# Building the token table: three buffers of 0/1 matrices, comparisons on pairs of fp16 values, and the narrow matrix ahead of the wide one

## The reference

```python
logits = xf @ gate_w.T + lb_bias
scores = sigmoid(logits); topw, topi = top_k(scores, 2)
topw = topw / (topw.sum(-1) + 1e-8)
for e in range(8):
    m = topi == e; sel = m.any(-1)
    wmean = (topw * m).sum() / max(m.sum(), 1)
    out += where(sel, mlp_e(xf) * wmean, 0)
out += mlp_shared(x)
```

## Time and profile before

| | |
|---|---|
| median of 3 runs | 992.47 us (992.27 to 993.35) |
| the profiled execution | 992.81 us, its span 991.0 us |
| mean granted TensorE clock | 0.988 |
| PE busy | 947.4 us (96%), 7136 matmuls |
| DVE busy | 699.7 us (71%) |
| ACT busy | 650.9 us (66%) |
| POOL busy | 350.6 us (35%) |
| L1197, `ohA` x16 | 15.2 us, mean 950 ns |
| L1201, `ohB` x16 | 10.2 us, mean 639 ns |
| L1360, `ohB` x16 on POOL | 702 / 706 / 1235 ns, shortest, median, longest |

### The profile page before, as it was taken

The page is one execution under the profiler, slowest core; times in us unless marked ns, Lnnn a source line. Parts: engine busy times, 40 slices in busy tenths (PEclk is TensorE's granted clock), DMA queues, the critical chain, the costliest instruction groups (busy, mean ns, idle before and its releaser), DMA issues.

```text
span 991.0 us, 20111 instructions
## 1 busy us (share of the span) xinstructions
PE 947.4 (96%) x7136; PEld 758.3 (77%) x7136; DVE 699.7 (71%) x2000; ACT 650.9 (66%) x1801; POOL 350.6 (35%) x349
## 2 busy tenths in 40 slices
PE   5679998889999999999999999999999999999998
PEld 4456776667788787888888888888878778777776
DVE  5779699786766657666575656666566786888884
ACT  3747667566767667676666766677666775677772
POOL 0231113453243253532434433444221444444441
PEclk9799999899999999999999999999999999999999
DMA  6486423553234435455354552547434442533421
GB/s 194 160 313 245 163 101 120 170 192 97 86 105 162 140 113 169 123 186 181 95 173 117 203 181 86 165 134 182 160 116 127 154 128 76 179 107 106 123 86 43
DMA packets 66002, 142.76 MB, mean 144 GB/s; under 512 B 7856, under 2 KB 40880, under 8 KB 64112
## 3 DMA queue, kind: packets, MB, share of 16 engines
q1 hardware_dynamic: 52896, 91.77, 28.3%
q0 software_dynamic: 12432, 49.29, 16.1%
q10 hardware_dynamic: 576, 0.42, 0.1%
HBM read 104.76 MB, written 36.70 MB: 143 GB/s over the span
## 4 chain that ended last, share of the span: by engine, by line
PE 84%; issue 7%; DVE 5%; POOL 2%; DMA 1%; ACT 1%; SPq 0%; DVEq 0%; POOLq 0%
PE PS L670 15%; PE PS L671 14%; PE PS L672 14%; PE PS L712 13%; PE PS L703 13%; PE PS L693 12%; PE PS L820 2%; POOL hh L1355 1%; DVE acc L986 1%; DVE pp L1242 1%; DMA xs<-xs_scratch 1%; PE PS L718 1%; POOL rstd L1347 1%; DMA xr<-in_w_moe 0%; DVE acc L1159 0%
## 5 line engine op out<-in xcount | busy, mean ns | idle before, releaser
L925 ACT ACTIVATE pp<-pp,nmax 128x128 f32<-128x128 f32 (+3 forms) x512 | 280.7, 551 | 97.4 <-DVE nmax L1242 97.4
L1242 DVE CUSTOM_DVE_ANT_0 pp<-PS,maskw 128x128 f32<-128x128 f32 (+3 forms) x512 | 215.2, 483 | 4.8 <-PE PS L693 3.4
L1403 POOL TENSOR_TENSOR yy<-yf,yy 128x512 fp32r<-128x512 f32 x63 | 82.4, 1307 | 278.9 <-ACT yy L861 278.5
L703 PE MATMUL PS<-ident,pp 128*128 128x128 f32 x1280 | 165.3, 276 | 0.1
L693 PE MATMUL PS<-qk 64*128 64x256 f32 (+2 forms) x1536 | 146.8, 337 | 15.3 <-issue 8.4
L703 PEld LDWEIGHTS PS<-ident,pp 128*128 128x128 f32 x1280 | 141.1, 140 | 14.9 <-issue 9.9
L712 PE MATMUL PS<-pt,vv 128*64 128x512 f32 (+3 forms) x1024 | 152.0, 439 | 0.0
L693 PEld LDWEIGHTS PS<-qk 64*128 64x128 f32 x1536 | 114.5, 191 | 31.0 <-issue 17.1
L712 PEld LDWEIGHTS PS<-pt,vv 128*64 128x64 f32 x1024 | 67.9, 136 | 90.3 <-issue 74.1
L861 ACT ACTIVATE pt<-PS 128x384 f32<-128x384 f32 (+1 forms) x215 | 108.5, 512 | 3.1 <-PE PS L703 3.1
L1248 DVE COPY pt<-PS 128x384 f32<-128x384 f32 x169 | 99.1, 591 | 12.7 <-PE PS L703 12.7
(11 more groups left out here) (166 smaller groups left out, 2051.7 us busy)
## 6 DMA issues: line engine op xcount, KB each, us to landing
rb<-rr_scratch SPq DMA_DIRECT2D x128, 128.0 KB
wr<-wm_scratch SPq DMA_DIRECT2D x16, 768.0 KB, 5.4
y_scratch<-acc SPq DMA_DIRECT2D x39, 256.0 KB
acc<-in_x SPq DMA_DIRECT2D x15, 512.0 KB, 5.4
wm_scratch<-hh SPq DMA_DIRECT2D x10, 768.0 KB, 4.0
xs_scratch<-wr SPq DMA_DIRECT2D x7, 1024.0 KB, 5.3
xs<-xs_scratch SPq DMA_DIRECT2D x7, 1024.0 KB, 4.7
xn_scratch<-acc SPq DMA_DIRECT2D x8, 512.0 KB, 3.1
```

What stands on the lines that cost most here:

```text
L703: done = e.transpose(o, pp[:, i % 4, P_AT[t] + 128 * kt:P_AT[t] + 128 * kt + 128], ident[:, :])
L925: e.activation(scores, scores, ACT.Exp, scale=-1.0, bias=nmax[:, b, t:t + 1], accum_out=rs[:, i % 4, 2 * t + h:2 * t + h + 1]).then_inc(a_ ...
L1242: e.tensor_tensor_reduce(pp[:, b, P_AT[t]:P_AT[t] + n], g[:, at:at + n], maskw[:, 512 - n:512], -1.0, 3e38, ALU.add, ALU.min, accum_out=nm ...
L1403: e.tensor_tensor(yy[:, i % 2, 1, :], yf[:, :], f32(yy[:, i % 2, 0, :]), ALU.subtract).then_inc(g_yl, 1)
```

## The change

`hi` and `lo` are written as fp16, every value twice side by side (`pairs`), and ACT makes an fp16 copy of the 128 numbers of `iota` once. Both comparisons then have 16-bit inputs, and their patterns end in a dimension of two neighbours. `ohB` is compared first, and POOL waits for it alone. Both matrices have three buffers; the three of `ohA` lie in the part of `acc` that held the routing's scratch `tot`, `pos` and `tri`, which is no longer read by then. `select` i waits for `tokens` i - 3. No piece moves in the order of the work.

```diff
-        hilo = sb("hilo", [128, 2, 64])
-        ohA = sb("ohA", [128, 2, 4, 128], F16)
-        ohB = sb("ohB", [128, 2, 4, 2 * NBLK], F16)
+        hi = sb("hi", [128, 64])
+        pairs = sb("pairs", [128, 2, 64, 2], F16)
+        iota16 = sb("iota16", [128, 128], F16)
+        ohB = sb("ohB", [128, 3, 4, 2 * NBLK], F16)
...
+        ohA = acc_flat[:, 2304:3072].bitcast(F16).rearrange("p (b c s) -> p b c s", b=3, c=4)
...
-                        done = e.matmul(g[:, 0:2 * NBLK], ohA[:, i % 2, c, :], ohB[:, i % 2, c, :], start=c == 0, stop=c == 3)
+                        done = e.matmul(g[:, 0:2 * NBLK], ohA[:, i % 3, c, :], ohB[:, i % 3, c, :], start=c == 0, stop=c == 3)
...
                     e.activation(rv("s"), lgf, ACT.Exp, scale=-1.0).then_inc(a_sig, 1)
+                    w.wait_ge(d_kc, 16)
+                    copy(iota16[:, :], iota).then_inc(a_iota, 1)
...
+            def twice(m):
+                return m[:, :].unsqueeze(2).to_broadcast([128, 64, 2])
...
-            ts(hi, hi, 12582912.0, None, ALU.subtract)
+            ts(hi2, twice(hi), 12582912.0, None, ALU.subtract)
...
-            e.scalar_tensor_tensor(lo, hi, -128.0, m12[:, :], ALU.mult, ALU.add).then_inc(v_ro, 1)
+            e.scalar_tensor_tensor(lo2, hi2, -128.0, twice(m12), ALU.mult, ALU.add).then_inc(v_ro, 1)
...
-                    if i >= 2:
-                        w.wait_ge(p_tk, i - 1)
-                    e.tensor_tensor(ohA[:, i % 2, :, :], iota.unsqueeze(1).to_broadcast([128, 4, 128]),
-                                    lo[:, 4 * i:4 * i + 4].unsqueeze(2).to_broadcast([128, 4, 128]),
-                                    ALU.is_equal).then_inc(v_sel, 1)
-
-                    e.tensor_tensor(ohB[:, i % 2, :, :], iota[:, 0:2 * NBLK].unsqueeze(1).to_broadcast([128, 4, 2 * NBLK]),
-                                    hi[:, 4 * i:4 * i + 4].unsqueeze(2).to_broadcast([128, 4, 2 * NBLK]),
-                                    ALU.is_equal).then_inc(v_sel, 1)
+                    w.wait_ge(a_iota, 1)
+                    if i >= 3:
+                        w.wait_ge(p_tk, i - 2)
+                    for o, n, slot in ((ohB, NBLK, hi2), (ohA, 64, lo2)):
+                        e.tensor_tensor(o[:, i % 3, :, :].rearrange("p c (s t) -> p c s t", t=2),
+                                        iota16[:, 0:2 * n].rearrange("p (s t) -> p s t", t=2).unsqueeze(1)
+                                        .to_broadcast([128, 4, n, 2]),
+                                        slot[:, 4 * i:4 * i + 4, :].unsqueeze(2).to_broadcast([128, 4, n, 2]),
+                                        ALU.is_equal).then_inc(v_sel, 1)
...
-                    w.wait_ge(v_sel, 2 * i + 2)
+                    w.wait_ge(v_sel, 2 * i + 1)
```

More of the change, by code:

```diff
@@ L334, in attention_moe_kernel @@
                                         "wo"))
-        a_wm, a_bt, a_tanh, a_hh, a_ys = (new_sem("a_" + n) for n in ("wm", "bt", "tanh", "hh", "ys"))
+        a_wm, a_bt, a_tanh, a_hh, a_ys, a_iota = (
+            new_sem("a_" + n) for n in ("wm", "bt", "tanh", "hh", "ys", "iota"))
         v_cst, v_wlo, v_st, v_mv, v_xn, v_xtl, v_lg, v_ro, v_tot, v_sel, v_tk, v_lat, v_q, v_k = (
@@ L450, in attention_moe_kernel @@
         m1, m2 = m12[:, 0:32], m12[:, 32:64]
-        hi, lo = hilo[:, 0, :], hilo[:, 1, :]
+        hi2, lo2 = pairs[:, 0, :, :], pairs[:, 1, :, :]
         lgf = lg[:, :, :].rearrange("p t e -> p (t e)")
@@ L1106, in route_ops @@
                 yield
-            ts(hi, m12[:, :], 1.0 / 128, -63.5 / 128, ALU.mult, ALU.add)
+            ts(hi[:, :], m12[:, :], 1.0 / 128, -63.5 / 128, ALU.mult, ALU.add)
             yield
-            ts(hi, hi, 12582912.0, None, ALU.add)
+            ts(hi[:, :], hi[:, :], 12582912.0, None, ALU.add)
             yield
-            ts(hi, hi, 12582912.0, None, ALU.subtract)
+            ts(hi2, twice(hi), 12582912.0, None, ALU.subtract)
             yield
             own()
-            e.scalar_tensor_tensor(lo, hi, -128.0, m12[:, :], ALU.mult, ALU.add).then_inc(v_ro, 1)
+            e.scalar_tensor_tensor(lo2, hi2, -128.0, twice(m12), ALU.mult, ALU.add).then_inc(v_ro, 1)
             yield
@@ L1357, in gpsimd_program @@
                 elif kind == "select" and lag == 1:
-                    o, n = ohB[:, i % 2, :, :], 4 * i % 32
-                    w.wait_ge(v_sel, 2 * i + 2)
+                    o, n = ohB[:, i % 3, :, :], 4 * i % 32
+                    w.wait_ge(v_sel, 2 * i + 1)
                     e.tensor_tensor(o, o, token[:, n:n + 4].unsqueeze(2).to_broadcast([128, 4, 2 * NBLK]),
```

## The result

| | before | after |
|---|---|---|
| median of 6 runs each, one chip | 992.61 us (991.65 to 993.35) | 988.76 us (987.46 to 990.12) |
| ratio | | 0.9963, 95% interval 0.9951 to 0.9974 |
| profiled execution, its span | 992.81, 991.0 us | 987.46, 985.6 us |

The change is worth 3.9 us by the medians (interval 2.6 to 4.9). The profiled execution of after is the fastest of its six and shows 5.4 us; what probably makes the difference is told under `again`.

What follows compares the result with a forecast made beforehand. PE was taken as bound by the weight-split chain to 197 us, DVE to 213, then a wait at 218 us with slow clock. 0.43 + 0.9 + 1.9 + 1.3 = 4.5 us off 992.47 gave 988.0 us, range 985.8 to 990.

Steps and rivals of the forecast that it cites:

- Cost of a comparison: DVE's two comparisons per select fall from 0.69 and 0.47 us to 0.41 and 0.31, 7 us of DVE time in 16.
- Writing the pairs: Two routing instructions on DVE handle 128 elements instead of 64, costing 0.12 us on the path before select 0.
- `ohB` first: POOL's product starts 0.6 us after select 0 instead of 1.15; less 0.12 for the pairs, 0.43 us gained.
- PE time gained between 181 and 196 us is given back at 196.86: PE's transposes at 196.86 stand behind the weight-split chain, so only an earlier start of that chain counts.
- Part one: The stretch to 197 us, limited by a chain through the weight split; it gains 0.43 us.
- the slow clock at 184 to 187 us: A slow stretch of PE's clock before 197 us, said to earn nothing.
- Part two: The stretch from 197 to 213 us, limited by DVE; it gains 0.9 us, all that PE waited there.
- Part three: PE's wait at 218.57 us for L1209 on DVE goes, through three buffers and shorter comparisons: 1.9 us gained.
- Clock: If PE doesn't idle near 218 us, the slow clock from 220 to 230 us goes: 1.3 us saved.
- Comparisons no faster: Rival, chance 0.14: DVE stays at 1.06 ns per element with 16-bit inputs; 0.9 us gained, 991.2 us.
- Something else holds PE at 218 us: Rival, chance 0.16: PE's 1.9 us idle and the slow clock behind it stay; 1.3 us gained, 991.1 us.
- the collision: Rival, chance 0.07: DVE's `ohA` waits out POOL's product in each of 16 selects; 3 us slower, 995.4 us.

Runs made afterwards that it cites:

- again: The kernel after once more, no line changed, on another chip: median 1007.42 us, ratio to before 0.9969.
- load_first: The kernel after, with SP loading the next raw expert matrix ahead of the store of the split one: 985.16 us, ratio to before 0.9927.
- two_buffers: The kernel after with two buffers in place of three: 1006.91 us, ratio to before on the same chip 0.9965.
- idle_218: The kernel after, with one `out_part` of PE made to wait for a late POOL instruction, a wait of 1.9 us: 992.15 us, ratio to before 1.0001.
- no_packing: The kernel after with fp32 comparisons instead of 16-bit pairs: 1008.46 us, ratio to before on the same chip 0.9981.
- spaced225: The kernel after with the next load ahead of the store and expert-weight splits planned 9 ticks apart instead of 8: 1007.77 us, ratio to before 0.9962.

## Why the prediction was right

988.0 us were forecast and 988.8 measured, in the forecast's own range. Part of that closeness is luck: the sum of 4.5 us was worked out on profiled executions, where 5.4 came out, and the median gained 3.9. By its steps, against the first profile:

**Cost of a comparison: right**, 0.41 and 0.31 us. The slope is (0.414 - 0.313) / 200 = 0.51 ns per element where it was 1.06. The Trainium skill, "VectorE: DVE Perf Modes", section "Mode 2×_1P — pack two bf16 into one 32-bit read", gives two results per cycle for 16-bit operands with adjacent neighbours. The runs agree, and show it for pairs of which one operand repeats its own.

**Writing the pairs: right within 0.1 us.** The two instructions take 0.23 and 0.29 us instead of 0.20 and 0.22. Select 0 began at 169.52 instead of 169.57, since the next comparison ended at POOL's release in both, so nothing came on the path.

**`ohB` first: right in kind, with 0.69 us for 0.43.** POOL's first product is recorded 0.39 us after select 0 and takes 0.82 us instead of 0.71. So it is held 0.11 us by `ohA`, not the 0.2 I allowed. 0.05 us of the shift was there before select 0.

**"PE time gained between 181 and 196 us is given back at 196.86": wrong.** This is the step that failed. I joined and the earlier trace rows because one ended as the other began. But the exponential of 196.08 belongs to pair 10, and the transposes of 196.86 to pair 9, whose exponentials were long done. In after PE's timeline has its transposes at 195.14:

```profile
195.14 1.28 PE L706 MATMUL PS<-ident,pp 128*128 128x128 f32 x10
```

and ACT's has the exponential behind them in time:

```profile
195.41 0.71 ACT L930 ACTIVATE pp<-pp,nmax 128x512 f32<-128x512 f32 x1
```

Part one gained 1.7 us, by the waits at 181.7, 184.0 and 190.4 us. What the chain really limits is `key` 11 near 197 us, through ACT's copy of a query, which had 1.3 us of slack before and is where PE waits 2.2 to 2.5 us whenever the load is late; and the last scores at 202.6 us, through ACT's evictions. With this step went its companion, that the slow clock at 184 to 187 us "lies in part one and earns nothing": it did stay in after, but in `load_first`, without it, PE's busy time is 2.67 us shorter.

**"Part two gains 0.9 us": wrong, nothing was gained.** The waits of 0.7 and 0.2 us are gone, and 0.8 us for ACT came at 202.62 instead. I had named ACT as late next, but behind the scores and not ahead of their last third. The two errors cancel by luck: both parts give 1.65 us together where 1.33 were forecast.

**Part three, 1.9 us: right**, 3.80 - 1.65 = 2.15. POOL's `yy` came at 211.96, select 14's `ohB` was held by it for 1.46 us, and L1209's successor came at 214.31, before PE arrived at 214.77: forecast were 212.4, 215.0 and 215.3. But the three buffers have no part in it: `two_buffers` has it as well.

**Clock, 1.3 us: right** for these two executions (5.16 - 3.80 = 1.36), and in `idle_218`; but two other profiles have such a wait and no slow clock.

**The rivals.** "Comparisons no faster" is `no_packing` by its time: 1.9 us won, forecast 1.3. "Something else holds PE at 218 us" and the collision did not occur in the first profile, where `ohA` was never behind POOL's product. In `again`, `load_first` and `spaced225` it was, where selects follow each other closely near 180 us (0.92 us instead of 0.41, once or twice each); `load_first` is the fastest kernel all the same. A late load, and so a median behind the profiled execution, was in none of them.

## What to carry to other kernels

An interval that two engines' timelines share is no dependence: before a gain is written off "because the next step starts as that one ends", check by name and number that it is the same tile's work, a pair ahead or behind. When several edits aim at one stall, measure them one at a time as well: here every part alone ended the slow clock behind one stall, and the sum of the single gains was about twice the whole. When a stage stops being the bound, follow the chain of waits again at once: it pointed at a load and a store in one queue, and exchanging them won as much as the change. And divide such a gain into idle and busy time of the same work before you explain it: here more than half of it was the clock, which the chain of waits doesn't show.

## What the runs showed of the hardware

In five profiles a single 16 KB packet of instruction loading (0.96 or 0.97 us, once 1.70, the time of one DMA engine) started 0.7 to 3.2 us behind the issue of a 384 KB load, and the load landed after 5.8 to 6.0 us, with its last packets one by one; in six it started 4.1 to 4.3 us behind, and the load took 4.6 to 4.7. That the packet is the cause is argued, not shown. The same load took 4.57 us beside a 768 KB store issued 0.37 us ahead of it, and 3.58 us when issued ahead of the store. A POOL product beside a DVE comparison of two SBUF inputs took 1.09 us by 0.68 us of comparison and 0.82 by 0.41, against 0.71 alone. The same 338 matmuls kept PE busy for 42 us at a full clock and for 46.5 at a mean granted clock of 0.90. Of four waits of PE of 1.9 to 2.0 us near 218 us, two were followed by half clock and two were not.
